# Waits for landings between GpSimd's row scatters in a two-layer model with a mixture of experts

## The reference

```python
x = x + _L0_attn_ref(_layernorm(x), ...)
x = x + _L0_ffn_ref(_layernorm(x), ...)
x = x + _L1_attn_ref(_layernorm(x), ...)
x = x + _L1_ffn_ref(_layernorm(x), ...)

# _L1_ffn_ref: n = 2048 tokens, D = 256, E = 64 experts, F = 64, K = 4
_, topk_idx = jax.lax.top_k(logits + router_bias, K)
combine = zeros(n, E).at[arange(n)[:, None], topk_idx].add(topk_scores)
g = jnp.einsum('nd,edf->enf', flat, Wg)
u = jnp.einsum('nd,edf->enf', flat, Wu)
hw = jax.nn.silu(g) * u * combine.T[:, :, None]
out = jnp.einsum('enf,efd->nd', hw, Wd)
for i in range(2):                       # shared experts, for every token
    out = out + (jax.nn.silu(flat @ Sg[i]) * (flat @ Su[i])) @ Sd[i]
```

## Time and profile before

| | us |
|---|---|
| timed runs, median of 3 | 1907.24 |
| timed runs, lowest and highest | 1905.54, 1908.77 |
| profiled execution, span from its first to its last instruction | 2028.0 |
| in it: first and last dispatch scatter start | 1597.02, 1679.01 |
| in it: first gather of sorted rows is issued | 1731.61 |
| in it: first and last result scatter start | 1759.18, 1993.37 |

### The profile page before, as it was taken

The page is one execution under the profiler, slowest core; times in us unless marked ns, Lnnn a source line. Parts: engine busy times, 40 slices in busy tenths (PEclk is TensorE's granted clock), DMA queues, the critical chain, the costliest instruction groups (busy, mean ns, idle before and its releaser), DMA issues. The chain is left out here.

```text
span 2028.0 us, 39275 instructions
## 1 busy us (share of the span) xinstructions
PE 1785.8 (88%) x14393; PEld 1508.3 (74%) x14393; DVE 1312.5 (65%) x2649; ACT 804.2 (40%) x1961; POOL 797.0 (39%) x1082
## 2 busy tenths in 40 slices
PE   5999999999999999984899999999996727588885
PEld 3888888888888888872688888888875516577773
DVE  5877787777777788877766666666764616233334
ACT  3444444444444444432455555555553202122221
POOL 3333533344333444433624324334342571145541
PEclk9999999999999999985999999999997758788886
DMA  2100010001960000001200101000002421644426
GB/s 92 48 0 0 0 48 0 0 0 51 348 4 0 1 1 0 0 0 37 74 1 1 43 1 43 1 1 2 2 2 82 173 105 40 174 134 145 153 100 236
DMA packets 72003, 108.83 MB, mean 54 GB/s; under 512 B 24096, under 2 KB 52640, under 8 KB 70976
## 3 DMA queue, kind: packets, MB, share of 16 engines
q1 hardware_dynamic: 61552, 77.59, 13.5%
q0 software_dynamic: 9168, 25.31, 3.2%
q10 hardware_dynamic: 1152, 4.19, 0.5%
HBM read 62.37 MB, written 44.96 MB: 53 GB/s over the span
## 5 line engine op out<-in xcount | busy, mean ns | idle before, releaser
L1820 POOL DMA_INDIRECT ys<-rows_yb,dest x127 | 122.2, 962 | 192.2 <-ACT rows_yb L2117 157.7
L846 POOL TENSOR_TENSOR a_ms<-a_ms,a_esq 128x4 f32<-128x4 f32 x64 | 14.4, 224 | 436.5 <-DVE a_ms L733 436.5
L1346 ACT ACTIVATE b_prob<-b_sc,b_nmax 128x128 f32<-128x128 f32 x256 | 99.8, 392 | 143.0 <-DVE b_nmax L1437 143.0
L1432 DVE SCALAR_TENSOR_TENSOR b_sc<-b_ps_s,window_mask 128x512 f32<-128x512 f32 x64 | 44.3, 692 | 121.6 <-PE b_ps_s L1225 121.6
L1199 PE MATMUL b_ps_u<-xh,b_w_hi 128*128 128x512 f32 x256 | 113.4, 443 | 3.1 <-DVE b_rope L1424 2.1
L602 DVE RECIPROCAL a_rz<-a_ps_sz 128x256 f32<-128x256 f32 x64 | 112.5, 1757 | 3.7 <-PE a_ps_sz L350 3.7
L2009 PE MATMUL t_ps<-t_wd,rows_hT 64*128 x256 | 79.4, 461 | 40.1 <-ACT rows_hT L2110 28.4
L561 ACT ACTIVATE a_sq<-a_ps_og 128x512 f32<-128x512 f32 x64 | 38.3, 598 | 176.3 <-PE a_ps_og L456 161.0
L1524 POOL TENSOR_TENSOR b_Q<-b_rope 128x512 f32<-128x512 f32 x32 | 41.2, 1287 | 161.6 <-DVE b_rope L1424 161.6
L1199 PE MATMUL b_ps_u<-xl,b_w_hi 128*128 128x512 f32 x256 | 101.5, 396 | 0.0
L1199 PE MATMUL b_ps_u<-xh,b_w_lo 128*128 128x512 f32 x256 | 101.2, 395 | 0.0
(11 more groups left out here) (352 smaller groups left out, 6150.7 us busy)
## 6 DMA issues: line engine op xcount, KB each, us to landing
xs<-a_zeros SPq DMA_DIRECT2D x32, 528.0 KB, 12.5
xn_all<-xs SPq DMA_DIRECT2D x32, 528.0 KB
wgu_all<-wgu SPq DMA_DIRECT2D x4, 2048.0 KB, 13.8
b_w_raw<-Wb SPq DMA_DIRECT2D x12, 512.0 KB, 5.0
wgu_all<-ys SPq DMA_DIRECT2D x8, 512.0 KB, 11.9
wgu_all<-ys ACTq DMA_DIRECT2D x8, 512.0 KB, 12.4
X<-x SPq DMA_DIRECT2D x2, 1024.0 KB, 7.0
a_w_raw<-Wv SPq DMA_DIRECT2D x4, 512.0 KB, 6.1
```

What stands on the lines that cost most here:

```text
L1346: last = nc.scalar.activation(prob[:, n % 2, h, :], sc[:, h % 2, h // 2, :], ACT.Exp, bias=nmax[:, at:at + 1], accum_out=den[:, n % 2, 0, ...
L1820: pool.indirect_dma_start(ys, bass.IndirectOffsetOnAxis(ap=dest[:, i % HOMES, j:j + 1], axis=0), yb[:, i % YR, j // 2, j % 2, :], None).th ...
```

## The change

Two waits are put into GpSimd's program. Ahead of every eighth dispatch scatter, the first excepted (scatters 8, 16, ..., 56: seven times), GpSimd waits until all the scatters before have landed. Ahead of the first result scatter of each group but the first (31 times) it waits until the group before has landed.

```diff
+        BURST = 8
...
                 for n in range(b * CH * TOPK, (b + 1) * CH * TOPK):
                     t, k = n // TOPK, n % TOPK
+                    if n and n % BURST == 0:
+                        pool.wait_ge(sent, 16 * n)
                     pool.indirect_dma_start(xs, ..., xn[:, t, :], None).then_inc(sent, 16)
             for i in range(NGRP):
                 for j in range(sends(i)):
                     if j == 0:
+                        if i:
+                            pool.wait_ge(y_sent[(i - 1) % YR], 64 * ((i - 1) // YR + 1))
                         pool.wait_ge(y_act, i + 1)
                     if j == 2:
                         pool.wait_ge(y_dve, i + 1)
                     pool.indirect_dma_start(ys, ..., yb[:, i % YR, j // 2, j % 2, :], None).then_inc(y_sent[i % YR], 16)
```

## The result

The changed kernel takes 1988.91 us (median of 4 runs, 1985.84 to 1990.80) against 1906.39 for the kernel before in the same comparison: a ratio of 1.043, 95% interval 1.0417 to 1.0442. It is 82.5 us slower. The forecast was slower, 1954, with a range of 1919 to 2000: direction and range hold, the cost was under-sized, 47 against 82.

A forecast was written before the change was run, and what follows sets the result against it. The prediction took GpSimd to bound dispatch, and TensorE and GpSimd in a dead heat the expert loop. Dispatch waits 9.5 plus result waits 37.8 made 47.3 us, 1907.2 to 1954.5, range 1919 to 2000.

The forecast's parts named there:

- The timed runs have none of the pauses: Dispatch and expert loop: unexplained engine pauses make the profiled execution some 121 us longer and are nearly absent when timed.
- the fully busy stretch: Ahead of the tail TensorE is busy 400.00 of 400 us at full clock, so the 121 us can't lie there.
- 2028.0 - 50.2 - 70.1: Profiled span less pauses in dispatch (50.2) and pauses with slow matmuls in the expert loop (70.1): 1907.7, against 1907.24 timed.
- Rival A: Dispatch and expert loop: pauses are in timed runs too and shorter scatter series remove them; faster, 1834 us, chance 0.10.
- GpSimd is the bound of dispatch, with no cover: Dispatch: the shared experts' slack covers none of the seven waits, 1.36 us each, so the gather starts 9.5 us later.
- The landing of 2.43 us and a step of 2.63: Each wait, both places: a scatter lands in 2.43 us, plus 0.20 wake-up; the step is 2.63 instead of 1.27.
- Results, 37.8 us: Expert loop: 31 waits lengthen GpSimd's group from 5.21 to 6.43 us, 1.22 each, 37.8 us in all.
- its upper bound: Expert loop: a gather ahead of each group's last scatter makes the landing 4.44 us; cost 110 us with dispatch, time 2017.
- Rival B: Both waits: the landing mostly fits in GpSimd's own step, or GpSimd has slack; no change, 1907 us, chance 0.08.
- rival C: Expert loop: TensorE's rests drop its clock, 71 us more, 2026; with the gather's collision, chance 0.10.
- The profile's span falls while the timed runs get slower: Whole kernel: the profiled execution's pauses may shrink, so its span may fall though timed runs slow; no size given.

The follow-up runs named there:

- dispatch_only: The kernel before with only the seven dispatch waits added, result scatters left as they were: 1917.82 us, ratio 1.0055.
- weights_after_gather: The kernel before with the last three loads of the expert weights (1.8 MB) issued after the first gather instead of ahead of it: 1911.11 us, ratio 1.0026.
- results_only: The kernel before with only the 31 waits of the result scatters added, dispatch left as it was: 1977.27 us, ratio 1.0374.
- gather_after_landing: The changed kernel with each gather from the tenth on held by SyncE until the landing that starts GpSimd's next group: 1963.24 us.
- two_waits: The changed kernel with a second wait in each group, ahead of its third result scatter, for the first two to land: 2014.95 us.

## Why the prediction was right, and where it was off

- **The timed runs have none of the pauses: right.** That was the step on which the sign hung, and it was read from the fully busy stretch and from 2028.0 - 50.2 - 70.1. Two new profiles of the same kernel, without pauses, have spans of 1907.1 and 1904.5, and none of the 47 recorded spans is above 1907.2. The agreement of that sum to 0.5 us was luck in part: its gather came 4.3 us too soon (84.4 us after the first scatter, 1597.02 to 1681.4, against 88.7 measured), its way from the gather to the first result scatter was left at 27.6 us, against 19.1, and the stages ahead of dispatch ended 3.1 us earlier in that execution (1597.02 against 1600.15): errors of -4.3, +8.5 and -3.1 that nearly cancel.
- **Rival A: out.** Its mechanism needs pauses that are there in each run. The cause of the pauses in that one execution stays open. They are not tied to the scatters or their pace, which the same kernel has twice more without a pause.
- **GpSimd is the bound of dispatch, with no cover: right.** In the new profile of the kernel before SyncE stands 14.4 us for the scatters, the shared experts being done. The cost was forecast at 9.5; dispatch_only measured 10.6. That they are so close hides opposite errors: the rests are some 6 us more than forecast (the sixth landing above all, amid the weight loads), the last landing gets 3.0 us shorter and the scatters' records 1.4.
- **The landing of 2.43 us and a step of 2.63: right where nothing else moves.** The last landings of dispatch in the changed kernel and in weights_after_gather took 2.44 and 2.50. Five of the seven dispatch waits rest 1.73 to 2.23 us, and six of the eight groups after the last gather take 6.41 to 6.53. Where other transfers were under way it failed, in the kernel before too: the last dispatch landing, put at 2.43, took 5.45. An estimate of 2.30 us for one DMA from the Trainium skill ("DMA: Bandwidth & Descriptors", "Anatomy of one DMA — SWDGE (gpsimd) path") agrees with the undisturbed landing of 2.44 within 0.14.
- **Results, 37.8 us: the term that was mis-sized.** It measured 69.8 in the profile and 70.1 in results_only. The prediction had the cause as its upper bound, a gather ahead of each last scatter (3.23 a group, against 2.25 measured), and set it aside in the sentence that puts the gather "just after GpSimd starts the next group, so it meets the group's first scatters and not its last". That sentence added up copy, TensorE's 5.2 us and `find_home` one after the other. But TensorE had run ahead before it had to wait for a buffer, its transposes were done, and only copies, the tanh with its products and `find_home` lay between: 3.0 us (1786.95 to 1789.92) in place of 7.2. gather_after_landing puts the gather about where the sentence had it, at the next group's start, and 25.7 us go. The range held because it was drawn up to a step of 3.6 us; the mean step between groups measured 3.66 (0.96 and 2.70 of rest), where the forecast had 2.63.
- **Rival B: out; rival C: its clock part isn't needed.** No wait of the changed kernel rests less than 1.66 us, so the landing doesn't fit in GpSimd's step. `down` does run at the lower of the clock's two levels, 1.2 of 2.4 GHz, in some groups (3.65 us at 1788.41, granted clock 0.51), but all 31 of GpSimd's waits end with a landing and none with a copy, and ScalarE stands 5.87 us for the landing at 1786.95: TensorE had time to spare. The other part of C, the gather's collision, did come, at about half its price (32 us against 110 - 47).
- **The profile's span falls while the timed runs get slower: right**, by 40.6 against +82.5.

## What to carry to other kernels

Set the span of the profile against the timed median before you look for what to mend: a pause that the timed runs don't have can't be won back, and a second profile of the same kernel costs less than a change. A wait for a DMA on the engine that issues it costs issue-to-landing less the engine's usual step each time (2.69 in place of 1.27 us here), unless it waits for something one step older, which cost nothing here. And price a landing with the transfers that are released by the same event in flight, from a timeline: which queue gets its go at that moment, and what had already been done ahead of it.

## What the runs showed of the hardware

One profiled execution of a kernel was 121 us longer than two later ones of the same kernel (2028.0 against 1907.1 and 1904.5), all of it between the first dispatch scatter and the last result scatter, with engines standing up to 26.75 us for nothing that the trace names.

From the issue of a scatter of 128 rows (131 to 135 KB) to GpSimd's next instruction behind its landing it took 2.63 to 2.69 us with no other transfer beside it, 3.6 to 4.9 in the eleven groups of the changed kernel whose gather of 0.54 MB was issued 1.0 us ahead of it (3.92 in the one shown), and 7.08 in the middle of 4.2 MB of loads. With the gather 2.4 us ahead (two_waits) it was back at 2.62 to 2.70 in 11 of 13 groups. A load of 16 KB of instructions, begun within 1.6 us behind the scatter, went with 3.15 to 3.95 us in four traces that had no gather there.
